# Probabilities times values: one fp32 product in place of three products of fp16 halves

## The reference, cut to what matters

```python
def xattn(q, k, v, attn_mask, Wq, Wk, Wv, Wo):        # q: layernorm(x); k, v: ctx
    qh, kh, vh = proj_heads(q, Wq), proj_heads(k, Wk), proj_heads(v, Wv)   # 16 heads of 64
    scores = jnp.einsum('bhqd,bhkd->bhqk', qh, kh) + attn_mask
    probs = jax.nn.softmax(scores, axis=-1)
    ctx = jnp.einsum('bhqk,bhkd->bhqd', probs, vh)
    return jnp.einsum('bse,de->bsd', ctx, Wo)
x = x + jnp.tanh(g_xattn[0]) * xattn(...)
h = jax.nn.relu(jnp.einsum('nd,edh->enh', layernorm(x), W1) + b1[:, None, :])
y = jnp.einsum('enh,ehd->end', h, W2) + b2[:, None, :]
x = x + jnp.tanh(g_ffn[0]) * jnp.einsum('end,ne->nd', y, comb)   # comb: top-2 softmax weights
```

## Time and profile before

| | |
|---|---|
| median of 3 runs | 1155.34 us (1152.26 to 1156.29) |
| the profiled execution: its time | 1155.76 us |
| its span, first to last instruction | 1154.0 us |
| PE busy | 1071.0 us, 93% |
| DVE busy | 973.1 us, 84% |
| ACT busy | 847.2 us, 73% |
| POOL busy | 793.6 us, 69% |
| mean granted clock of the PE | 0.965 of full speed |

### The profile page before, as it was taken

One profiled execution on the slowest core, in us unless ns is written; L12 is line 12 of the kernel. 1 busy time (PEld: TensorE's weight loads), 2 busy tenths in 40 slices (PEclk: granted clock), 3 DMA queues, 4 the chain that ended last, 5 costly groups with the idle time before them and its releaser, 6 DMA issues.

```text
span 1154.0 us, 36397 instructions
## 1 busy us (share of the span) xinstructions
PE 1071.0 (93%) x13921; PEld 785.2 (68%) x13921; DVE 973.1 (84%) x1935; ACT 847.2 (73%) x1553; POOL 793.6 (69%) x719
## 2 busy tenths in 40 slices
PE   6889898989989899998989989899998989999986
PEld 4457576767767676776767767676676767768665
DVE  5798898988979888897988979888898987888777
ACT  4878686868767787786867767687686867878765
POOL 3768576767757677676767757677676767779853
PEclk9889899999989999998999999899999999999998
DMA  8223212212222122222212222122222212212100
GB/s 201 49 54 69 62 39 56 48 38 48 57 42 43 38 59 46 50 45 49 55 34 52 52 45 45 38 54 51 47 48 53 51 27 41 48 29 56 22 11 19
DMA packets 123163, 56.91 MB, mean 49 GB/s; under 512 B 26584, under 2 KB 122864, under 8 KB 122992
## 3 DMA queue, kind: packets, MB, share of 16 engines
q1 hardware_dynamic: 122992, 54.59, 22.4%
HBM read 16.80 MB, written 4.19 MB: 18 GB/s over the span
## 4 chain that ended last, share of the span: by engine, by line
PE 61%; DVE 17%; issue 10%; POOL 8%; ACT 3%; DMA 1%; DVEq 0%; ACTq 0%; SPq 0%; POOLq 0%
PE bank L43 18%; PE bank L44 17%; PE bank L45 17%; PE bank L315 3%; DVE x2hat L643 3%; POOL hidL L884 2%; POOL ptL L921 2%; PE bank L263 2%; PE bank L300 2%; POOL rstd L869 2%; DVE comb L857 1%; DVE picked L845 1%; ACT qH L466 1%; DVE otL L782 1%; DVE vL L734 1%
## 5 line engine op out<-in xcount | busy, mean ns | idle before, releaser
L884 POOL TENSOR_TENSOR hidL<-hid,hidH 128x512 f16<-128x512 f32 x242 | 279.7, 1169 | 19.8 <-ACT hidH L496 19.6
L921 POOL TENSOR_TENSOR ptL<-pt,ptH 128x512 f16<-128x512 f32 x128 | 148.4, 1159 | 151.7 <-ACT pt L557 151.5
L466 ACT ACTIVATE qH<-bank 128x512 f16<-128x512 f32 x256 | 153.6, 605 | 75.6 <-PE bank L45 74.7
L43 PE MATMUL bank<-w2H,hidH 128*128 128x128 f16 x1024 | 187.9, 225 | 7.1 <-DVE hidL L769 4.4
L927 POOL TENSOR_TENSOR prob<-prob,row_inv 128x512 f32<-128x512 f32 x128 | 133.8, 1045 | 84.3 <-DVE row_inv L763 84.3
L44 PE MATMUL bank<-w2L,hidH 128*128 128x128 f16 x1024 | 187.5, 225 | 0.0
L45 PE MATMUL bank<-w2H,hidL 128*128 128x128 f16 x1024 | 187.2, 225 | 0.0
L486 ACT ACTIVATE hid<-bank,b1col 128x512 f32<-128x512 f32 x256 | 181.4, 709 | 7.9 <-PE bank L45 6.4
L496 ACT ACTIVATE hidH<-bank,b1col 128x512 f16<-128x512 f32 x256 | 183.6, 717 | 0.0
L651 DVE TENSOR_TENSOR qL<-bank,qH 128x512 f16<-128x512 f32 x224 | 152.5, 681 | 27.5 <-ACT qH L466 27.4
L43 PE MATMUL bank<-ptH,vdH 128*128 128x64 f16 x1024 | 118.8, 201 | 44.1 <-DVE x L716 43.0
(11 more groups left out here) (144 smaller groups left out, 3696.0 us busy)
## 6 DMA issues: line engine op xcount, KB each, us to landing
vdH<-vH SPq DMA_DIRECT2D x256, 64.0 KB, 2.1
vdL<-vL SPq DMA_DIRECT2D x256, 64.0 KB, 2.1
x_raw<-in_x SPq DMA_DIRECT2D x16, 256.0 KB, 3.5
ctx_raw<-in_ctx SPq DMA_DIRECT2D x16, 256.0 KB, 3.5
mask_raw<-in_fside_Bx1xSxS SPq DMA_DIRECT2D x32, 128.0 KB, 2.9
out_x<-x SPq DMA_DIRECT2D x16, 256.0 KB, 2.5
qH<-in_L_xattn_Wq SPq DMA_DIRECT2D x1, 512.0 KB, 5.9
qH<-in_L_xattn_Wk SPq DMA_DIRECT2D x1, 512.0 KB, 7.9
```

Source lines behind the costliest of these rows:

```text
L43: e.matmul(dst, lhs[0], rhs[0], start=start, stop=False, skip_group_check=True)
L466: act.activation(qH[:, g % 2, 2 * j + g2, :, h2, :], bk("Q", g, h)[:, :].rearrange("p (b q) -> p b q", b=GB), ACT.Copy).then_inc(s_q_high, 1)
L884: pool.tensor_tensor(hidL[:, m % 2, c, :], hid[:, k % NR, :], hidH[:, m % 2, c, :], ALU.subtract).then_inc(s_hid_low[c], 1)
L921: pool.tensor_tensor(ptL[:, b % 2, :], pt[:, b % 2, :], ptH[:, b % 2, :], ALU.subtract).then_inc(s_pt_low, 1)
```

## The change

The values are evicted once, in fp32, to `v`, and the turned probabilities once, in fp32, to `pt`. The low halves and their instructions go: `vL` on DVE, `ptH` on ACT, `ptL` on POOL. SP moves one fp32 tile of values in place of two fp16 tiles: two transfers for each step in place of four, each twice as large. PV becomes one fp32 product for each head pair. The waits on `v_low` and `pt_low` become waits on ACT's evictions.

```diff
-        ptH, ptL = (sb(f"pt{p}", [P, 2, N], F16) for p in "HL")
-        vH, vL = (sb(f"v{p}", [P, 2, C // CL, DV, CL], F16) for p in "HL")
-        vdH, vdL = (sb(f"vd{p}", [P, 2, 2, C // CL, 2, DV, CL], F16) for p in "HL")
+        v = sb("v", [P, 2, C // CL, DV, CL])
+        vd = sb("vd", [P, 2, 2, C // CL, 2, DV, CL])
...
-                pe.wait_ge(s_pt_low, b + 1)
+                pe.wait_ge(s_pt_out, b + 1)
...
-                    lhs = [v[:, t % 2, b % 2, c // CL, :, :, c % CL].rearrange("p g d -> p (g d)") for v in (vdH, vdL)]
-                    last = three_passes(pe, bk("PV", b)[:, cols], lhs, (ptH[:, b % 2, cols], ptL[:, b % 2, cols]))
+                    last = pe.matmul(bk("PV", b)[:, cols],
+                                     vd[:, t % 2, b % 2, c // CL, :, :, c % CL].rearrange("p g d -> p (g d)"),
+                                     pt[:, b % 2, cols], start=True, stop=True, skip_group_check=True)
...
-                    act.activation(vH[:, g2, :, :, :].rearrange("p a d c -> p (a d c)"), bk("V", t, g2)[:, :],
-                                   ACT.Copy).then_inc(s_v_high, 1)
+                    act.activation(v[:, g2, :, :, :].rearrange("p a d c -> p (a d c)"), bk("V", t, g2)[:, :],
+                                   ACT.Copy).then_inc(s_v_out, 1)
...
-                    act.activation(ptH[:, b % 2, :], bk("PT", b)[:, :], ACT.Copy).then_inc(s_pt_high, 1)
-                    if b >= 2:
-                        act.wait_ge(s_pt_low, b - 1)
                     act.activation(pt[:, b % 2, :], bk("PT", b)[:, :], ACT.Copy).then_inc(s_pt_out, 1)
...
-                    dve.tensor_tensor(vL[:, g2, :, :, :].rearrange("p a d c -> p (a d c)"), bk("V", t, g2)[:, :],
-                                      vH[:, g2, :, :, :].rearrange("p a d c -> p (a d c)"),
-                                      ALU.subtract).then_inc(s_v_low, 1)
...
-                    pool.tensor_tensor(ptL[:, b % 2, :], pt[:, b % 2, :], ptH[:, b % 2, :],
-                                       ALU.subtract).then_inc(s_pt_low, 1)
...
-                    for src, dst in ((vH, vdH), (vL, vdL)):
-                        for b2_ in range(2):
-                            sp.dma_start(dst[g2 * S:(g2 + 1) * S, t % 2, b2_, :, g2].rearrange("p a d c -> p a (d c)"),
-                                         src[b2_ * S:(b2_ + 1) * S, g2].rearrange("p a d c -> p a (d c)")
-                                         ).then_inc(s_place[t % 2][g2], 16)
+                    for b2_ in range(2):
+                        sp.dma_start(vd[g2 * S:(g2 + 1) * S, t % 2, b2_, :, g2].rearrange("p a d c -> p a (d c)"),
+                                     v[b2_ * S:(b2_ + 1) * S, g2].rearrange("p a d c -> p a (d c)")
+                                     ).then_inc(s_place[t % 2][g2], 16)
```

More of the change, by code:

```diff
@@ L152, in flamingo_block @@
             sem(n) for n in ("weights_high", "xT_high", "ctxT_high", "x2T_high"))
-        s_q_high, s_v_high, s_exp, s_pt_high, s_pt_out, s_o_high = (
-            sem(n) for n in ("q_high", "v_high", "exp", "pt_high", "pt_out", "o_high"))
+        s_q_high, s_v_out, s_exp, s_pt_out, s_o_high = (
+            sem(n) for n in ("q_high", "v_out", "exp", "pt_out", "o_high"))
         s_q_out = [sem(f"q_out{i}") for i in range(2)]
@@ L163, in flamingo_block @@
         s_q_low = [sem(f"q_low{i}") for i in range(2)]
-        s_v_low, s_max, s_shift, s_sum, s_inv, s_o_low, s_res = (
-            sem(n) for n in ("v_low", "max", "shift", "sum", "inverse", "o_low", "residual"))
+        s_max, s_shift, s_sum, s_inv, s_o_low, s_res = (
+            sem(n) for n in ("max", "shift", "sum", "inverse", "o_low", "residual"))
         s_scaled, s_b2_add, s_y_tail, s_hid_tail = (sem(n) for n in ("y_scaled", "b2_add", "y_add_tail", "hid_low_tail"))
@@ L176, in flamingo_block @@
         s_q_pool = [sem(f"q_low_pool{i}") for i in range(2)]
-        s_pt_low, s_normal, s_y_add, s_before, s_above = (
-            sem(n) for n in ("pt_low", "normal", "y_add", "rank_before", "rank_add"))
+        s_normal, s_y_add, s_before, s_above = (
+            sem(n) for n in ("normal", "y_add", "rank_before", "rank_add"))
         s_hid_low = [sem(f"hid_low{c}") for c in range(HC)]
@@ L210, in placed @@
         def placed(t, g2):
-            return s_place[t % 2][g2], 64 * (t // 2 + 1)
+            return s_place[t % 2][g2], 32 * (t // 2 + 1)
         taken, bank_of = [], {}
@@ L226, in evicted @@
             if kind == "V":
-                return [(s_v_low, 2 * at[0] + at[1] + 1)]
+                return [(s_v_out, 2 * at[0] + at[1] + 1)]
             if kind == "scores":
@@ L230, in evicted @@
             if kind == "PT":
-                return [(s_pt_high, at[0] + 1), (s_pt_out, at[0] + 1)]
+                return [(s_pt_out, at[0] + 1)]
             if kind == "PV":
@@ L730, in _ @@
                     queries_low(g + 1, 2 * i)
-                if within(s // 2, TILES):
-                    t, g2 = s // 2, s % 2
-                    dve.wait_ge(s_v_high, s + 1)
-                    dve.tensor_tensor(vL[:, g2, :, :, :].rearrange("p a d c -> p (a d c)"), bk("V", t, g2)[:, :],
-                                      vH[:, g2, :, :, :].rearrange("p a d c -> p (a d c)"),
-                                      ALU.subtract).then_inc(s_v_low, 1)
                 m = s - 3 - FFN_LAG
@@ L895, in _ @@
             pool.memset(minus_half[:, :], -0.5).then_inc(s_half, 1)
-            pool.memset(vdH[:, :, :, :, :, :, :], 0.0).then_inc(s_vzero, 1)
-            pool.memset(vdL[:, :, :, :, :, :, :], 0.0).then_inc(s_vzero, 1)
+            pool.memset(vd[:, :, :, :, :, :, :], 0.0).then_inc(s_vzero, 1)
             pool.wait_ge(s_half, 1)
@@ L1017, in _ @@
                     if t == 0:
-                        sp.wait_ge(s_vzero, 2)
+                        sp.wait_ge(s_vzero, 1)
                     if t >= 2:
                         sp.wait_ge(s_pv, 2 * t - 2)
-                    sp.wait_ge(s_v_low, s + 1)
-                    for src, dst in ((vH, vdH), (vL, vdL)):
-                        for b2_ in range(2):
-                            sp.dma_start(dst[g2 * S:(g2 + 1) * S, t % 2, b2_, :, g2].rearrange("p a d c -> p a (d c)"),
-                                         src[b2_ * S:(b2_ + 1) * S, g2].rearrange("p a d c -> p a (d c)")
-                                         ).then_inc(s_place[t % 2][g2], 16)
+                    sp.wait_ge(s_v_out, s + 1)
+                    for b2_ in range(2):
+                        sp.dma_start(vd[g2 * S:(g2 + 1) * S, t % 2, b2_, :, g2].rearrange("p a d c -> p a (d c)"),
+                                     v[b2_ * S:(b2_ + 1) * S, g2].rearrange("p a d c -> p a (d c)")
+                                     ).then_inc(s_place[t % 2][g2], 16)
             sp.wait_ge(s_store[0], 16 * GROUPS // 2)
```

## The result

| | median | runs |
|---|---|---|
| before | 1155.82 us | 1152.26 to 1157.04, 4 runs |
| changed | 1538.13 us | 1535.4 to 1540.73, 4 runs |
| ratio | 1.331 | 95% interval 1.328 to 1.335 |

The changed kernel is 382 us slower. The direction was forecast; the size was not: 1270 was predicted, and the range ended at 1350.

The account below looks back on a forecast made before the run. The prediction took the PE's stream, plus one DVE-made gap in a group, as the bound: 1155.8 + 122 (PV) - 6 (gap) - 2 (first two groups) = 1270 us, forecast 1250 to 1290, range 1165 to 1350.

Parts of the forecast that it names:

- PE as the bound: Whole kernel: the time is the PE's instruction stream, busy 93% of the span, plus one DVE-made gap in a group.
- two records for a product: PV: each of eight true fp32 products takes two records of load and product, 16 records for each sequence.
- 128 times PV's growth on the path: PV on the PE: 0.95 us more for each of 128 sequences, +122 us, all on the PE's path.
- the gap at L716 that stays: PV's first product at the change from step 5 to 6: PE still waits for DVE's L716, some 40 us in 14.
- the transfers and shorter chain that are worth nothing: Value transfers twice as large still land long before PV; PV's 1.8 us shorter chain isn't waited for; both worth nothing.
- 0.109 us a record: PV on the PE: price of an fp32 record at full clock, taken from records that move 128 columns.
- PV after: PV as eight fp32 products: 16 x 0.109 = 1.74 us for each sequence, against 0.79 before.
- A: Rival on PV's weight load: the 16-byte distance between weights makes it dearer than forecast, the milder case; chance 0.15.
- B: Rival on PV's weight load: the 16-byte distance between weights makes it dearer, beyond A; chance 0.08.
- what goes: Removed DVE, ACT and POOL work: nothing in mid-group, -6 us at the gap, -2 us in the first two groups.
- The gap's mechanism: DVE's `x2hat` before L716 run faster without POOL's `ptL` beside them: 0.44 us in each of 13 groups, -6 us.
- the 2 us: First two groups, without experts: short PE waits in which PV's growth may hide, -2 us.

## Why the prediction was wrong

**What held.** PE as the bound; two records for a product; 128 times PV's growth on the path, with nothing beside it to hide it; the gap at L716 that stays, though with 22 us of waiting in all where some 40 were forecast; the transfers and shorter chain that are worth nothing. The direction, and what happens with neighbouring columns: 0.109 us a record was forecast, and 0.111 measured.

**The term that failed** is "PV after": 16 x 0.109 = 1.74 us. It was 3.57. The 0.109 is the price of the turnings that move 128 columns; that PV's records run at it too was the author's estimate, and no run shows it for weights 16 bytes apart. The runs show 0.111 us with neighbouring columns, 0.118 at 8 bytes and 0.233 at 16. The prediction saw the distance, and gave 0.15 (A) and 0.08 (B) of the chance to a load that it makes dearer. B, the dearer one, is what happened. What the forecast did wrong was to scale from the fp16 row: 20 ns more at 8 bytes, 118 against 98, was read as a slope. It isn't one: in fp32 it is 6 ns more at 8 bytes and 134 more at 16, and what fp16 pays at 8 bytes says nothing about 16. That put the term 234 us too low: 128 x (3.57 - 1.74).

**A term that was missing** is the clock: 1538.1 - 1463.5 = 75 us. The prediction had the lower clock only as a thing behind idle time, which is what the rows of before showed.

**A term that was mis-sized** is what goes: -8 was forecast, -38 measured with an unchanged PE stream. The gap's mechanism was right. The size took 0.58 us as the price of a DVE operation without POOL beside it, from `xhat`. But POOL was working beside those too, for 1.72 of their 2.32 us (592.06 to 593.78), so 0.58 is itself a mixture. Two rows of the kernel before, and two of the changed one:

```profile
591.62 1.05 POOL L927 TENSOR_TENSOR prob<-prob,row_inv 128x512 f32<-128x512 f32 x1
592.62 1.16 POOL L884 TENSOR_TENSOR hidL<-hid,hidH 128x512 f16<-128x512 f32 x1
```

```profile
601.61 2.09 DVE L640 TENSOR_SCALAR xhat<-x_raw,meanvar,rstd 128x128 f32<-128x128 f32 x4
...
606.10 2.91 DVE L640 TENSOR_SCALAR x2hat<-x,meanvar,rstd 128x128 f32<-128x128 f32 x4 [1.13 <-POOL rstd L860]
```

Four `xhat` take 2.09 us in place of 2.32 and four `x2hat` 2.91 in place of 3.77, 1.1 us in a group, not 0.44. In the run without low halves the PE waits 28.1 us for this in place of 44.6, which is 16 of the 38. The shorter gap also has less of the lower clock behind it: 39 us of that run are at the lower level, 81 before (0.983 and 0.965 over the span), worth up to half of the difference, 21 us, by estimate. And the first two groups gave more than the 2 us.

**The sum again**, from the kernel before: 1155.8 + 356 (PV) + 75 (clock) - 38 (removed work) = 1549, against 1538.1 measured. The 11 us left over are not assigned; longer steps hide more of the idle time in the first two groups (PE busy 81.92 of 82.00 us from 45 to 127 in the changed kernel, 76.31 without low halves), which is 6 of them. With neighbouring columns the same sum is 1155.8 + 128 x (1.73 - 0.79) - 38 = 1238, and 1237.7 was measured (1.73 from the rows at 600.43 and 602.16); with one record of reduced fp32 it is 1155.8 + 128 x (8 x 0.111 - 0.79) - 38 = 1130, and 1125.9 was measured. This last one is close partly by luck: with the 1.00 us that the rows show in place of 8 x 0.111 it is 1145. But there the first record starts 0.03 us behind the product before it, and not the 0.22 that the others leave (600.22 to 600.43 with neighbouring columns in true fp32), so 1.00 isn't all added time either.

## What to carry to other kernels

When a product's weights change their type, look at how many bytes lie between two columns, not how many elements: the same layout of 4 elements cost 18 ns a load in fp16 (8 bytes, 118 ns against 100) and doubled the price of every record in fp32 (16 bytes, 0.233 us against 0.111). For products with few moved columns, cost the weight load first; here it was the whole price, and 64 more moved columns were free (0.233 us a record with 64 as with 128). And split a change like this: evicting once was worth 3% by itself, and the product lost it nine times over.

## What the runs showed of the hardware

- Loads of 128 fp32 columns take 194, 200 and 328 ns at distances of 4, 8 and 16 bytes, and records follow at 0.111, 0.118 and 0.233 us. In fp16, 100 ns at 2 bytes and 118 at 8.
- Records with the slow load (328 ns) follow at the same 0.233 us at either level of the granted clock, 1.00 and 0.50, and in true fp32 as in the reduced type; with half the weights' columns at 0.12.
- The granted clock was 0.930, 0.954 and 0.985 over the span with 64, 96 and 128 columns moved past the same loads, 1538, 1510 and 1463 us. With 64 it fell with the PE busy for at least 8 us in 44 of 58 stretches, with 128 in none of 13. More work through the array made the kernel 5% faster. With half as many of these records (reduced fp32, 64 columns, 1.87 us for each sequence) the clock was 0.981 and fell only behind idle time of the PE.
- `x2hat` on DVE, fp32 from SBUF to SBUF, takes 946 ns with POOL busy beside it and 757 with POOL busy for part of the time.
